# Cross-attention and mixture of experts on one core: the place of the score pairs in TensorE's order

## The reference, cut to what matters

```
x: (4, 512, 512), ctx: (4, 512, 256); 16 heads of 32
q = ln(heads(layernorm(x) @ Wq + bq))
main: the 496 first rows of ctx, dca: the 16 last rows of ctx
k, v         = ln(heads(main @ Wk + bk)), heads(main @ Wv + bv)
k_dca, v_dca = the same of dca @ Wkv_dca + bkv_dca
ctx = softmax(q k^T / sqrt(32)) v  +  softmax(q k_dca^T / sqrt(32)) v_dca
x = x + ctx @ Wo + bo
x = x + moe(layernorm(x))        # 7 routed experts, top 2, and a shared one
```

## Time and profile before

| | |
|---|---|
| three executions | 993.09, 993.65, 998.34 us; median 993.65 |
| profiled execution | 995.3 us, its span 993.6 us, mean TensorE clock 0.962 of full |
| TensorE busy | 909.5 us, 92% |
| VectorE | 636.0 us, 64% |
| GpSimd | 563.9 us, 57% |
| ScalarE | 459.5 us, 46% |
| L1089 exponentials | 256 of 595 ns, 138.9 us |
| L1136 maxima in `attend` | 60 of 2231 ns, 133.9 us |
| L1212 score products | 256 of 401 ns |
| L1219 values | 512 of 639 ns |

### The profile page before, as it was taken

One profiled execution on the slowest core, in us unless ns is written; L12 is line 12 of the kernel. 1 busy time (PEld: TensorE's weight loads), 2 busy tenths in 40 slices (PEclk: granted clock), 3 DMA queues, 4 the chain that ended last, 5 costly groups with the idle time before them and its releaser, 6 DMA issues. The chain is left out here.

```text
span 993.6 us, 16827 instructions
## 1 busy us (share of the span) xinstructions
PE 909.5 (92%) x5047; PEld 406.6 (41%) x5048; DVE 636.0 (64%) x1019; ACT 459.5 (46%) x846; POOL 563.9 (57%) x487
## 2 busy tenths in 40 slices
PE   3889895799999999989999689999999999999898
PEld 1345442122221222246644245555555555555443
DVE  7888777588787988467776144554554444443388
ACT  3375665678877888722353022332233233323540
POOL 5465556367777775543127499989999920000372
PEclk9798998599999999999999799999999999999999
DMA  7234635445454532133425766666566643335676
GB/s 233 77 92 122 179 105 166 139 158 169 167 177 159 177 105 70 53 107 128 153 112 218 289 191 209 217 200 220 201 215 205 201 139 106 121 109 187 232 203 221
DMA packets 106059, 162.26 MB, mean 163 GB/s; under 512 B 12536, under 2 KB 55608, under 8 KB 105616
## 3 DMA queue, kind: packets, MB, share of 16 engines
q1 hardware_dynamic: 92768, 115.86, 35.9%
q0 software_dynamic: 12896, 45.10, 13.6%
q10 hardware_dynamic: 336, 0.57, 0.2%
HBM read 107.88 MB, written 53.48 MB: 162 GB/s over the span
## 5 line engine op out<-in xcount | busy, mean ns | idle before, releaser
L1089 ACT ACTIVATE p_t<-a_psT 128x512 f32<-128x512 f32 x256 | 138.9, 595 | 47.4 <-PE a_psT L1212 46.1
L1136 DVE TENSOR_REDUCE nm<-quad 128x4 bf16<-128x1984 f32 x60 | 133.9, 2231 | 35.7 <-PE quad L1197 35.7
L1905 ACT ACTIVATE e_xT<-quad 128x512 f16<-128x512 f32 x38 | 22.7, 597 | 229.9 <-PE quad L1969 229.9
L1979 PE MATMUL quad<-w_exp,e_xT 128*128 x456 | 107.2, 386 | 4.9 <-DVE e_xT L1933 2.6
L1039 POOL TENSOR_TENSOR p_sum<-p_t,p_t 128x512 f32<-128x512 f32 x64 | 81.1, 1275 | 53.2 <-ACT p_t L1089 53.0
L1979 PE MATMUL quad<-w_exp,e_uT 128*128 x456 | 104.6, 379 | 0.0
L1979 PE MATMUL e_psY<-w_exp,e_gT 128*128 x456 | 104.6, 379 | 0.0
L1212 PE MATMUL a_psT<-q_stk,k_stk 98*128 98x512 f16 x256 | 84.6, 401 | 11.2 <-ACT p_t L1089 9.4
L215 POOL TENSOR_TENSOR w_exp<-e_raw,w_exp 128x1024 f16<-128x1024 f32 x42 | 91.7, 2184 | 3.5
L1936 DVE SCALAR_TENSOR_TENSOR e_g<-quad,bias 128x512 f32<-128x512 f32 x38 | 26.3, 691 | 85.4 <-PE e_psGT L1969 80.5
L1936 DVE SCALAR_TENSOR_TENSOR e_u<-quad,bias 128x512 f32<-128x512 f32 x38 | 26.3, 691 | 73.9 <-PE quad L1979 73.9
(11 more groups left out here) (338 smaller groups left out, 1797.0 us busy)
## 6 DMA issues: line engine op xcount, KB each, us to landing
xs_dram<-zero SPq DMA_DIRECT2D x38, 256.0 KB, 6.9
bias<-in_L_ffn_bup_dram SPq DMA_DIRECT2D x38, 256.0 KB, 3.3
bias<-in_L_ffn_bgate_dram SPq DMA_DIRECT2D x38, 256.0 KB, 3.4
ys_dram<-e_y SPq DMA_DIRECT2D x38, 256.0 KB, 2.0
e_x<-xs_dram SPq DMA_DIRECT2D x36, 256.0 KB, 2.8
q_dram<-q_st SPq DMA_DIRECT2D x24, 256.0 KB, 3.0
k_dram<-k_st SPq DMA_DIRECT2D x24, 256.0 KB, 3.6
q_stk<-q_dram SPq DMA_DIRECT2D x64, 96.0 KB
```

The source lines that it names most:

```text
L1089: act.activation(probs(w, k), psT[:, k % 2], ACT.Exp, scale=SCALE / (QS * QS)).then_inc(s["exp"], 1)
L1136: dve.tensor_reduce(nm[:, i, :, 0:1].rearrange("p h o -> p (h o)"), psS[:, :, 0:NMAIN], AX.X, ALU.max, negate=True)
L1979: ins = pe.matmul(dst[:, :], stationary, moving, start=(k == 0), stop=(k == len(terms) - 1))
```

## The change

Five score pairs move up in TensorE's written order: T01 past S2, T10 past the last sums, T11 past V2 and S3, T20 past dca, T21 past V3. T30 stays at the end.

```diff
                 if scored(old):
                     third_sums(old)
+                turned_pair(now, 0, 1)
                 if scored(new) and new:
                     scores(new, 2)
-                turned_pair(now, 0, 1)
+                turned_pair(now, 1, 0)
                 if scored(old):
                     last_sums(old)
-                turned_pair(now, 1, 0)
+                turned_pair(now, 1, 1)
                 if scored(old):
                     values(old, 2)
                 if scored(new) and new:
                     scores(new, 3)
-                turned_pair(now, 1, 1)
+                turned_pair(now, 2, 0)
                 if scored(old):
                     dca(old)
-                turned_pair(now, 2, 0)
+                turned_pair(now, 2, 1)
                 if scored(old):
                     values(old, 3)
-                turned_pair(now, 2, 1)
                 turned_pair(now, 3, 0)
```

## The result

The changed kernel takes 1000.11 us (median of 7 runs, 998.44 to 1001.12); the kernel before, run again beside it, 995.80 us (7 runs). The ratio is 1.0048 with a 95% interval of 1.0033 to 1.0062: slower by 4.3 us. The profiled execution of the changed kernel took 1001.12 us with a span of 999.3, against 993.6 before: 5.7 us more.

A forecast was written before the change was run, and what follows sets the result against it. TensorE and VectorE were taken to bound the head-group loop almost equally, 8.38 against 8.34 us over one stretch. Thirteen periods +5.66, end +0.38, start -1.38, clock +0.3 gave +4.96 on 993.65: 998.6 us, range 988 to 1006.

The forecast's parts named there:

- VectorE's chain: VectorE's work from a period's fourth maxima score run to the next period's second: 8.34 us, against TensorE's 8.38 before.
- the margin of 0.04 us: From the fourth maxima score run to the next second one, TensorE's 8.38 us and VectorE's 8.34 differ by only 0.04.
- The wait before X: Before the product that turns the maxima: the closed gap's 0.72 us returns as a wait for VectorE's second-attention scaling.
- The gap at T10: At the third score pair, now parted from the second only by a maxima score run: 0.39 us added per period.
- S2 behind T01: Third maxima score run now follows the second score pair: 0.54 us more, 3.41 us after the second run, not 2.87.
- The loads: Late loads in periods 3 to 10: their 5.9 us taken as gone, the longer period nearly matching SyncE's queue.
- Start and end: First period of the head groups saves 1.38 us, less 0.3 for the clock; the last group adds 0.38.
- The sum: Over the head-group stage: 5.66 + 0.38 - 1.38 + 0.3 = +4.96 us, passed on in full to 998.6 us.
- B: Rival: in the head groups TensorE's closed gap is given back, not slower: 988.0 us; chance 0.12.
- C: Rival: TensorE's clock falls in each period after new waits: 1013 us, or 1006 in half the periods; chance 0.12.
- D: Rival: loads land as late behind TensorE as before, keeping the 5.9 us: 1004.5 us; chance 0.13.

The follow-up runs named there:

- S3 early: Kernel before with TensorE's score pairs reordered to close its gap, the fourth maxima score run moved earlier instead of later: 993.21 us, ratio 0.9983.
- The parts: Two TensorE orders: the earlier order's first part with the change's rest, 995.74 us; the changed order with the third maxima score run put back, 1004.19 us.
- thinner clears: SyncE's expert-buffer clears issued three a group instead of four: in the kernel before 990.79 us, in the changed kernel 1000.16 us.
- S3 early, thinner clears: Kernel before with both the S3 early order and the thinner clears: 988.11 us, ratio 0.9925.
- changed, VectorE's order altered: Changed kernel with VectorE's reciprocal and turned inverses moved ahead of the period's fourth maximum: 992.84 us, ratio 0.9976.
- S3 early, thinner clears, VectorE altered: Kernel before with S3 early, thinner clears, and VectorE's reciprocal and inverses moved ahead of the fourth maximum: 989.02 us, ratio 0.9929.

## Why the prediction was right

**VectorE's chain (right).** S3 to S1 was predicted at 8.34 and is 8.35. The chain is exact because it was read from one period, and its undisturbed end from the one place where VectorE alone decided. Altering VectorE's order alone took the wait before X away. Period 9 shows the margin of 0.04 us once more. There L1160 follows L1151 after 1.17 us instead of 0.81, in every kernel in which it stands right behind it. Those 0.36 us lengthen the period by 0.32 in the kernel before, by 0.35 in the changed one, and by 0.01 to 0.02 with S3 early, where TensorE sets S3 to S1.

**The wait before X (right in time, its latency mis-sized).** X comes 4.75 us after S3, predicted 4.65: from L1160's end (237.53) to X (237.68) pass 0.15 us, not the 0.05 taken from the S products. That costs nothing, since VectorE's L1165 is still behind it; V0 and S1 waited as written (0.35 measured before S1, 0.33 predicted).

**The gap at T10 (right sign, 0.10 too small).** This is the term of the sum that was mis-sized. The prediction took the price of adjacency as 1.79 (T21 to X) less two pairs of 0.535, but X follows a pair after 0.44 and not after 0.535, so the price there was 0.82. In front of a run of sums the same two pairs take 1.88, again 0.81 over two pairs. S2 to S3 is 3.88, not 3.78, and 13 periods make 1.3 us of it. That X follows sooner than a run of values does is seen at 248.59 and 249.03 above.

**S2 behind T01 (right in sum, wrongly addressed).** The 0.54 us was booked to S2's place. The parts show that it is the count of pairs ahead of S3 that counts: four instead of three.

**The loads (right in effect, the queue misread).** The 5.9 us were taken as gone. Of them 5.6 are; the other 0.3 was never a load but VectorE's late L1160 in period 9 (the earlier trace rows itself), and the changed kernel has it too. The thinner clears show the size of the loads from the other side, 4.5 us by the medians. The reason given was that SyncE's queue loses only 0.25 us a period against the longer loop. In fact it loses nothing: it now waits for TensorE, 0.7 to 2.7 us at a time and several times a group. SyncE's timeline, changed kernel:

```profile
257.85 0.45 SPq L1017 DMA_DIRECT2D k_hi<-k_dram  x1
260.38 0.73 SPq L1021 DMA_DIRECT2D q_stk<-q_dram  x1
```

Before, from 233 to 325 us, it had no pause over 0.15 us. Its clears (L1023) took a median of 1.48 us to issue between 230 and 325 us, and 0.73 in the changed kernel, so its pace of 15.78 us a group was not fixed. Why an issue takes longer there stays open.

**Start and end (right within 0.5 us).** The first period was 1.38 us shorter in the sum. S1 of period 2 came at 194.42 against 195.74 in the earlier trace rows, 1.32 earlier (1.55 if the stage's start, 0.23 later in this execution, is taken off). The clock rose in time for the sums in both, so the 0.3 us set aside for that were not needed. That is luck of the execution: with the same instructions on TensorE the first values of period 2 took 3.64 us in the kernel before and 2.37 with the thinner clears, since the clock rose at another moment (granted clock from 193 to 196 us 0.50 and 0.89). At the end the values, not the maximum rows, now set the sums, as predicted:

```profile
405.06 0.40 PE L1197 MATMUL quad<-k_hi,q_hi 32*128 32x512 f16 x4
...
411.13 1.92 PE L1219 MATMUL a_psO<-p_t,v_all 128*32 128x512 f32 x16 [0.51 <-DVE r_main L1165]
412.88 1.04 PE L1219 MATMUL a_psX<-p_sum,ones 128*32 128x512 f32 x8
```

S3 to the sums is 412.88 - 405.06 = 7.82, predicted 8.01, 8.56 before. (The 1.94 us taken for two runs of values held some wait: they take 1.86 from 250.48 to 252.34 above.)

**The sum.** Predicted +4.96, measured +5.7 by the spans and +4.3 by the medians. The parts hit less well than the total: the 13 periods cost 7.14 us and not 5.66, by the T10 term and the 0.3 of period 9, and the start (0.5 more saved), the end (0.1) and the work behind the stage (about 0.4 shorter, unexplained) gave most of it back, which is partly luck. The predicted 998.6 us stood on a median of 993.65 from three runs; with seven the kernel before is at 995.80, and that shift of 2.1 us is more than the distance of 1.5 to the measured 1000.11.

**The rivals.** B fell, by the waits for VectorE; the busiest engine's gap was closed and the loop grew. The rule of the Trainium skill (Perfetto Trace Analysis, Identifying Performance Opportunities) that the most occupied engine is the one to improve did not hold for this gap as the change closed it: that lost 4.3 us, and the same TensorE order gained only once VectorE's order released X earlier. Closed without delaying S3, the same gap gave 0.22 us a period. C fell: the granted clock of periods 3 to 10 was 1.00 with waits of 0.75, 0.35 and 0.24 us in each. D fell: no late loads. Its support was also a little thinner than written: in the kernel before SyncE's queue is solid from about 233 to 325 us, which is periods 5 to 10 and not 4 to 11.

## What to carry to other kernels

In a software pipeline where two engines' loops are equal within a few hundredths of a microsecond, closing a gap on one returns nothing by itself (a "release" below is the instruction that another engine waits for, here S3 for VectorE); first add up the other's chain between the two places where it is released (here S3 to S1), and move no work ahead of the release. When an order has to delay a release, look for idle time on the waiting engine ahead of it and shift that engine's independent work there, as the reciprocals ahead of S3's maximum. Separate such a comparison from load stalls, since a longer period can hide them and halve the visible loss.

## What the runs showed of the hardware

From the end of a VectorE instruction to a TensorE product that waits for it pass 0.05 to 0.06 us where the product is an S (L1137 ends at 241.22, S1 starts at 241.28) or V0 (238.95 and 239.00), and 0.15 us where it is X (237.53 and 237.68). Why X takes longer was not tested.

TensorE's clock fell to 1.2 GHz behind some late loads and not behind others. In this list a plus joins two waits within 4 us. The values behind took 2.89 to 3.51 us after waits of 0.56 + 1.15 and 1.27 + 0.76 (the kernel before), 1.88 + 0.51 and 1.58 + 0.48 (S3 early), and 1.73 alone (S3 early, thinner clears). They kept their 1.92 us after 1.41 + 0.30 (changed, VectorE's order altered), 1.22 (S3 early) and 1.44 alone (S3 early, thinner clears, VectorE altered), and in the changed kernel's every period of 0.75 + 0.35. So the cost that C names was real, but no fall followed the waits that the change makes.

In period 9 L1160 comes 0.36 us late behind L1151 in all eight kernels in which it stands right behind it. Where VectorE sets S3 to S1 and no load is late, that period is 0.32 to 0.36 us longer than its neighbours (15.97 against 15.62, 14.96 against 14.64, 15.50 against 15.15, 16.31 against 15.96); with S3 early it is not (14.43 against 14.42). Neither TensorE's order nor the clears touch the delay itself. What it is stays open.
